# A four-layer graph network on one core: relation scores in rounded halves, a new set-up and new orders on every engine

## The chip, the cores and the metric

The kernel runs on one core of one Trainium2 chip. A core has five engines with queues of their own: TensorE (PE; its weight loads are shown apart as PEld), VectorE (DVE), ScalarE (ACT), GpSimd (POOL) and SyncE (SP), which issues the DMAs here. Each works its queue in order and waits on semaphores. Only PE multiplies matrices; it writes to PSUM, which has eight banks of 128 x 512 float32. The metric is the device time of one execution in microseconds; the median of several runs counts.

## The reference, cut to what matters

128 graphs of 128 nodes with 256 features pass four residual layers, each on `h = relu(layernorm(x))`:

```python
# L0: attention of 8 heads under the adjacency mask, projection, layer norm added to itself
attn = softmax(where(adj == 0, -inf, q @ k.T * scale)); o = (attn @ v) @ w_proj + b_proj
x = x + o + layernorm(o) * gamma + beta
# L1: relation scores
q, k, v = h @ Wq.T, h @ Wk.T, h @ Wv.T
rel = adj.T * (q @ k.T)
rel = rel / norm(rel, axis=2, keepdims=True)
x = x + rel @ v
# L2: graph attention
g = h @ W
e = leaky_relu((g @ a1)[:, :, None] + (g @ a2)[:, None, :], 0.2) * adj
x = x + elu(softmax(e) @ g + beta * g)
# L3
x = x + (adj @ h) @ weight + bias
```

All arrays are float32.

## The kernel before

The graphs go in 64 pairs. The work on a pair is cut into stages, and a loop over steps `t` runs eight streams: in step `t` an engine works on pair `t` in stream 0 (`p0`), pair `t - 1` in stream 1 (`p1`), and so on to `p7`. Each engine has a function `step(t, par, on)` in which its operations stand in an order written out by hand, and `run(eng, step, set_up)` calls the steps; a pair `(t, make)` in its list calls the set-up function `make` ahead of step `t`. Every operation waits for its inputs by a count on a semaphore (`done`), for the last reader of a buffer that it overwrites (`wait_before`), and on PE for its PSUM bank (`bank_free`).

**Products.** A matrix product of two float32 operands is made in one of two ways. `product` (its matmuls stand on L314) takes operands that are split into a rounded high half and a rounded low half (`parts`, float32r) and adds three passes, hi times hi, hi times lo, lo times hi. It makes q, k, v, the projection, g, v1, hw and y, always with 256 or 258 moving columns. The other way is a plain float32 matmul, which appears as two instructions each: scores (L358), heads and their sums (L370, L374), rel times v (L417), u (L488), y_t (L520) and the relation scores (L458), and the transposes, which appear as one.

**The relation scores.** L1 folds Wq and Wk into one matrix when it starts (`fold`, L384), so that rel is h times g with g = w_qk times h. In before, ScalarE copies g out of PSUM as float32 (`g_t`, L650), and PE multiplies:

```python
last = pe.matmul(rel_bank[:, b * N:(b + 1) * N], h_t1_full[:, c, b * N:(b + 1) * N],
                 g_t[:, c, b * N:(b + 1) * N], start=c == 0, stop=c == C - 1)
```

four matmuls of 128 columns for a pair. `h_t1_full` is the float32 copy; its halves `h_t[1]` exist too, for g and v1.

**Normalising.** `moments` (VectorE: L706, L710) takes mean and variance, `inverse_root` (GpSimd: L901, L903) the inverse root, `normalize` (VectorE, L725) makes z. For L3 it is ScalarE instead: VectorE makes a shift, and ScalarE makes h in one operation with scale and bias (L590). PE transposes z, ScalarE makes the high half, VectorE the low one (`relu_lo`).

**The leaky slope.** ScalarE adds the two score vectors (Identity with bias, L612) into `e_sum`, VectorE makes `e_leaky` as the greater of the sum and 0.2 times the sum (L770), GpSimd multiplies with the adjacency (L942).

**Set-up.** SP issues x of pair 0, w_qkv, adj, w_q, w_k, x of pair 1, then the constants (`CONSTS`, the last one gamma) and the late constants (`LATE_CONSTS`, the last one w_out). ScalarE makes the high half of w_qkv in one piece, VectorE the low half. `fold` is called ahead of PE's step 0, `copy_fold` ahead of ScalarE's. VectorE makes the low half of the folded matrix ahead of its step 2, and GpSimd splits the other weights ahead of its step 2 (`next_constants`, `last_constants`).

Of the kernel before, what the change touches and what calls it, by code (L numbers as in the profile page):

```python
# [6 lines left out]
def gnn_stack(nc, x, adj, adj_t, w_qkv, w_proj, b_proj, gamma, beta_ln, w_q, w_k, w_v_t,  # L7
# [4 lines left out]
    ALU = mybir.AluOpType  # L12
# [16 lines left out]
    STREAMS = 8  # L29
# [5 lines left out]
    with ctx:  # L35
# [63 lines left out]
        rstd = sb("rstd", [128, NORMS, 2])  # L99
        shift3 = sb("shift3", [128, 2])  # L100
# [20 lines left out]
        g_t = sb("g_t", [128, C, 2 * N])  # L121
# [7 lines left out]
        e_sum = sb("e_sum", [128, 2, N])  # L129
# [21 lines left out]
        q_bank = mid[:, 2]  # L151
        k_bank = bank4[:]
        v_bank = bank7[:]
        p0_bank = mid[:, 0]
        p1_bank = bank5[:]
        p2_bank = bank7[:]
        p3_bank = bank4[:]
        heads_bank = bank5[:]
        sums_bank = mid[:, 0]
        o_bank = mid[:, 0]  # L160
        z1_bank = bank6[:]
        g_bank = bank6[:]
        v1_bank = bank6[:]
        rel_bank = mid[:, 3]
        rel_v_bank = bank4[:]
        z2_bank = mid[:, 2]
        hw0_bank = bank6[:]
        hw1_bank = mid[:, 2]
        s2_bank = mid[:, 1]
        att_bank = bank4[:]  # L170
        u_bank = mid[:, 1]
        y_t_bank = bank7[:]
        y_bank = bank5[:]
# [5 lines left out]
        mask_made, folded, folded_ready = sem("mask_made"), sem("folded"), sem("folded_ready")  # L179
# [8 lines left out]
        o_hi_ready, o_lo_ready = sem("o_hi_ready"), sem("o_lo_ready")  # L188
        q_psum, k_psum, v0_psum = sem("q_psum"), sem("k_psum"), sem("v0_psum")
# [5 lines left out]
        o_norm_ready, o_psum, o_ready = sem("o_norm_ready"), sem("o_psum"), sem("o_ready")  # L195
# [6 lines left out]
        hw_psum, hw_ready, s2_psum, e_sum_ready = sem("hw_psum"), sem("hw_ready"), sem("s2_psum"), sem("e_sum_ready")  # L202
# [47 lines left out]
        def flat(tile):  # L250
# [9 lines left out]
            (w_q_sb, w_q.rearrange("(c p) n -> p c n", p=128), fold_in),  # L260
            (w_k_sb, w_k.rearrange("(c p) n -> p c n", p=128), fold_in),
# [18 lines left out]
        def _(sp):  # L280
# [4 lines left out]
            for dst, src in CONSTS:  # L285
                sp.dma_start(dst, src).then_inc(const_in, 16)
            for dst, src in LATE_CONSTS:
                sp.dma_start(dst, src).then_inc(late_const_in, 16)

            def step(t, par, load, store):  # L290
                pb, p_out = t - 2, t - 7
# [6 lines left out]
                if store:  # L298
                    i = (par + 7) % 2
# [3 lines left out]
            for t in range(PAIRS + 7):  # L303
                step(t, t % 2, 2 <= t < PAIRS + 2 - 2, t >= 7)
# [4 lines left out]
        def _(pe):  # L309
# [69 lines left out]

            def fold():  # L380
                pe.wait_ge(fold_in, 16 * 2)
                for j in range(C):
                    for c in range(C):
                        last = pe.matmul(bank4[:, j * D:(j + 1) * D], w_q_sb[:, c, j * 128:(j + 1) * 128],  # L384
                                         w_k_sb[:, c, :], start=c == 0, stop=c == C - 1)
                last.then_inc(folded, 1)
                pe.wait_ge(fills_made, 3)
                pe.wait_ge(w_hi_ready, 2)
                pe.wait_ge(w_lo_ready, 1)

            def next_weights():
                pe.wait_ge(const_in, 16 * len(CONSTS))
                pe.wait_ge(split_ready, 2 * len(SPLIT))
                pe.wait_ge(w_lo_ready, 2)
# [6 lines left out]
            def step(t, par, on):  # L401
                p0, p1, p2, p3, p4, p5, p6, p7, p8 = [t - s for s in range(STREAMS + 1)]

                if on[1]:
                    pe.wait_ge(h_lo_ready[0], done(p1))
                    bank_free(pe, (hw_ready, p5, 2), (h_lo_ready[2], p5, 1), (max_ready[2], p2, 1))
                    columns(q_bank, w_qkv_p, 0, h_t[0]).then_inc(q_psum, 1)
                if on[3]:
                    pe.wait_ge(z_ready[1], done(p3))
                    bank_free(pe, (hw_ready, p5, 2), (v1_ready, p4, 1), (g_ready, p4, 1))  # L410
# [580 lines left out]
```

## Time and profile before

| | |
|---|---|
| median of 3 runs | 1473.15 us (1472.97 to 1476.63) |
| the profiled execution | 1474.63 us |
| its span, first to last instruction | 1472.8 us |
| PE, DVE, ACT, POOL busy | 98%, 86%, 77%, 51% of the span |
| granted TensorE clock, mean | 0.995 |

Busy time of an engine is the time in which at least one of its instructions runs; matmuls overlap one another, so their durations don't add up. The chain of work that ended last is PE for 95% of the span.

### The profile page before, as it was taken

What the parts mean: (1) busy time and instruction counts of PE and PEld (TensorE: products, weight loads), DVE (VectorE), ACT (ScalarE), POOL (GpSimd) and SP (SyncE); (2) the same over time, 40 slices, a digit from 0 to 9 for tenths busy, and PEclk for the clock granted to TensorE, in tenths of its full rate; (3) what the DMA queues carried; (4) which work ended last, traced back from release to release, by engine and by line L of the source; (5) the groups of instructions that cost most, each with busy time, mean ns of one, the idle gap of its engine ahead of it and who ended that gap; (6) DMA issues with size and microseconds to landing.
All of it is one profiled execution on the core that took longest, in us unless ns stands there. A gap on an engine that the chain in (4) does not pass through costs nothing.

```text
span 1472.8 us, 47814 instructions
## 1 busy us (share of the span) xinstructions
PE 1438.2 (98%) x16136; PEld 1370.3 (93%) x16136; DVE 1273.4 (86%) x5774; ACT 1134.7 (77%) x2884; POOL 748.4 (51%) x1107
## 2 busy tenths in 40 slices
PE   5999999999999999999999999999999999999996
PEld 5899999999999999999999999999999999999985
DVE  4889988988989889889889889889889889889885
ACT  4778878878877877877877778778778788788753
POOL 3455555555555555555555555555555555555452
PEclk9999999999999999999999999999999999999998
DMA  3000000100000000001001000000001001000000
GB/s 111 17 17 23 31 16 30 31 16 31 30 17 31 30 16 31 28 19 31 24 23 30 23 24 30 24 24 31 23 24 30 23 24 30 19 28 31 9 23 30
DMA packets 38113, 39.90 MB, mean 27 GB/s; under 512 B 2416, under 2 KB 37488, under 8 KB 37872
## 3 DMA queue, kind: packets, MB, share of 16 engines
q1 hardware_dynamic: 37872, 36.84, 7.9%
q8 instruction: 133, 2.18, 0.6%
q14 instruction: 108, 0.88, 0.2%
HBM read 20.05 MB, written 16.78 MB: 25 GB/s over the span
## 4 chain that ended last, share of the span: by engine, by line
PE 95%; DVE 1%; ACT 1%; issue 1%; POOL 0%; DMA 0%; SPq 0%; POOLq 0%; ACTq 0%; DVEq 0%
PE bank L314 34%; PE mid L314 15%; PE bank L349 6%; PE mid L358 5%; PE bank L520 5%; PE bank L370 4%; PE mid L458 4%; PE mid L374 4%; PE bank L330 4%; PE mid L488 4%; PE bank L417 4%; PE mid L330 2%; PE mid L349 2%; PE mid L493 1%; PE mid L527 1%
## 5 line engine op out<-in xcount | busy, mean ns | idle before, releaser
L546 ACT ACTIVATE probs<-masked,neg_max 128x128 f32<-128x128 f32 x1024 | 326.3, 395 | 6.3 <-DVE neg_max L716 6.3
L903 POOL TENSOR_TENSOR rstd<-var_eps,minus_half 128x2 f32<-128x2 f32 x320 | 240.9, 753 | 25.5
L716 DVE CUSTOM_DVE_ANT_0 masked<-mid,mask 128x128 f32<-128x128 f32 x1024 | 234.9, 286 | 6.9 <-issue 6.8
L915 POOL TENSOR_TENSOR xb<-x,b_proj_beta 128x512 f32<-128x512 f32 x64 | 81.9, 1279 | 233.9 <-DVE o_res L828 233.9
L901 POOL TENSOR_TENSOR var_eps<-mean_var,eps 128x2 f32<-128x2 f32 x320 | 63.5, 198 | 243.0 <-DVE mean_var L710 242.7
L706 DVE BATCH_NORM_STATS2 stats<-x 128x6 f32<-128x256 f32 x384 | 143.3, 415 | 0.1
L725 DVE TENSOR_SCALAR z<-x,mean_var,rstd 128x256 f32<-128x256 f32 x384 | 134.5, 405 | 7.1 <-POOL rstd L903 6.7
L946 POOL TENSOR_TENSOR h_t_lo<-h_t_full,h_t_hi 128x512 fp32r<-128x512 f32 x64 | 82.0, 1282 | 79.4 <-ACT h_t_hi L629 79.4
L349 PE MATMUL bank<-ident,probs 128*128 128x128 f32 x768 | 117.6, 276 | 4.9 <-ACT probs L546 4.9
L942 POOL TENSOR_TENSOR e_mask<-e_leaky,adj_sb 128x256 f32<-128x256 f32 x64 | 46.8, 731 | 116.2 <-DVE e_leaky L770 116.2
L370 PE MATMUL bank<-probs_t,v 128*32 128x128 f32 x2048 | 104.5, 276 | 0.3 <-issue 0.3
L770 DVE SCALAR_TENSOR_TENSOR e_leaky<-e_sum 128x256 f32<-128x256 f32 x64 | 27.3, 426 | 88.7 <-ACT e_sum L612 88.7
L374 PE MATMUL mid<-probs_t,ones 128*32 128x128 f32 x2048 | 103.0, 273 | 0.0
L604 ACT ACTIVATE ln_sum<-mid 128x512 f32<-128x512 f32 x64 | 38.2, 597 | 80.5 <-PE mid L374 80.5
L349 PEld LDWEIGHTS bank<-ident,probs 128*128 128x128 f32 x768 | 91.1, 147 | 6.2 <-ACT probs L546 6.2
L710 DVE BATCH_NORM_AGGREGATE mean_var<-stats 128x2 f32<-128x6 f32 x640 | 77.8, 163 | 13.8
L919 POOL TENSOR_TENSOR x3b<-x_up,b_out_less 128x512 f32<-128x512 f32 x64 | 82.6, 1290 | 11.3 <-DVE x L824 11.3
L314 PE MATMUL bank<-w_out_hi,y_t_hi 128*128 128x256 f32 x256 | 79.4, 310 | 6.9 <-DVE y_t_lo L778 6.9
L716 DVE DVE_READ_ACCUMULATOR2_ANT neg_max<- 128x1 f32 x1024 | 84.6, 83 | 0.0
L950 POOL TENSOR_TENSOR o_t_lo<-o_t,o_t_hi 128x512 fp32r<-128x512 f32 x64 | 83.0, 1298 | 3.1 <-ACT o_t_hi L633 3.1
L358 PEld LDWEIGHTS mid<-k_t,q_t 32*128 32x128 f32 x2048 | 63.0, 186 | 22.7 <-issue 20.2
L783 DVE SCALAR_TENSOR_TENSOR x<-bank,inv_norm,x 128x256 f32<-128x256 f32 x128 | 56.1, 480 | 28.8 <-PE bank L417 28.8
(156 smaller groups left out, 5725.8 us busy)
## 6 DMA issues: line engine op xcount, KB each, us to landing
x<-in_x SPq DMA_DIRECT2D x64, 256.0 KB, 2.7
out_x<-x SPq DMA_DIRECT2D x64, 256.0 KB, 2.1
w_qkv_sb<-in_w_qkv SPq DMA_DIRECT2D x1, 768.0 KB, 4.4
w_q_sb<-in_w_q SPq DMA_DIRECT2D x1, 256.0 KB, 4.4
w_k_sb<-in_w_k SPq DMA_DIRECT2D x1, 256.0 KB, 4.6
w_v_sb<-in_w_v_t SPq DMA_DIRECT2D x1, 256.0 KB, 5.8
w_proj_sb<-in_w_proj SPq DMA_DIRECT2D x1, 256.0 KB, 6.0
w_gat_x<-in_w_gat SPq DMA_DIRECT2D x1, 256.0 KB, 7.2
```

The costliest lines, as they stand in the source:

```text
L314: last = pe.matmul(dst, pick_l(lhs_t[a], c), pick_r(rhs[b], c), start=n == 0, stop=n == len(terms) - 1)
L330: last = pe.transpose(dst[:, (c * 2 + b) * N:(c * 2 + b + 1) * N], src[:, b, c * 128:(c + 1) * 128], ident[:])
L349: last = pe.transpose(dst[:, s * N:(s + 1) * N], probs[:, r, s], ident[:])
L358: last = pe.matmul(mid[:, r, s * N:(s + 1) * N], q_t[at, hc, b * N:(b + 1) * N], k_t[at, hc, b * N:(b + 1) * N], start=True, stop=True, ti ...
L370: pe.matmul(heads_bank[at, to], v0[:, b, hc * RG + r], probs_t[:, r, s], start=True, stop=True, tile_position=(0, r * HD))
L374: last = pe.matmul(sums_bank[at, to], ones[:], probs_t[:, r, s], start=True, stop=True, tile_position=(0, r * HD))
L546: last = act.activation(probs[:, r, s], masked[:, r, s], ACT.Exp, scale=-1.0, bias=neg_max[:, r, s:s + 1])
L706: dve.bn_stats(stats[:, k, b], src[:, b]).then_inc(ln_stats[k], 1)
L716: last = dve.tensor_tensor_reduce(out=masked[:, r, s], in0=mid[:, r, s * N:(s + 1) * N], in1=mask[:], scale=1.0, scalar=LARGE, op0=ALU.add ...
L725: last = dve.tensor_scalar(z[k][:, b], src[:, b], mean_var[:, k, b, 0:1], rstd[:, k, b:b + 1], ALU.subtract, ALU.mult)
L903: pool.tensor_tensor(rstd[:, k], var_eps[:, k], minus_half[:], ALU.pow).then_inc(ln_rstd[k], 1)
L950: pool.tensor_tensor(o_t_p[1][:], o_t[:], o_t_p[0][:].bitcast(f32), ALU.subtract).then_inc(o_lo_ready, 1)
```

## The change

- **Relation scores.** g gets halves too (`g_t_p`): ScalarE copies the rounded high half, VectorE subtracts it for the low half (`g_lo_ready`), and PE makes rel with `product`: twelve rounded matmuls of 128 columns in place of four in float32.
- **Leaky slope on ScalarE.** One Prelu with bias and slope makes `e_leaky`; `e_sum` and VectorE's operation go.
- **First z on ScalarE.** VectorE makes a shift of 128x2, and ScalarE makes z of L0 with Identity, scale and bias.
- **Set-up.** w_q and w_k are issued behind the constants. The halves of w_qkv are made in three pieces. `fold_low` (the low half of the folded matrix) and GpSimd's set-up are called ahead of step 0. PE waits ahead of step 0 for the weights, then folds; the folded matrix is made in the bank of the first score group, and step 0's scores wait until it is copied.
- **Orders.** The order on PE, ScalarE, VectorE and GpSimd is written anew, with other banks; the scores of a pair are made in stream 0 of PE (before: 1), z of L1 is transposed in stream 2 (before: 3), rel times v is in stream 3 (before: 4). With `STREAMS = 9` the sum into x4 and its store come one step later.

```diff
-    STREAMS = 8
+    STREAMS = 9
...
-        g_t = sb("g_t", [128, C, 2 * N])
+        g_t_p = parts("g_t", [128, C, 2 * N])
...
-            (w_q_sb, w_q.rearrange("(c p) n -> p c n", p=128), fold_in),
-            (w_k_sb, w_k.rearrange("(c p) n -> p c n", p=128), fold_in),
+        ]
+        FOLD_CONSTS = [
+            (w_q_sb, w_q.rearrange("(c p) n -> p c n", p=128)),
+            (w_k_sb, w_k.rearrange("(c p) n -> p c n", p=128)),
...
             for dst, src in CONSTS:
                 sp.dma_start(dst, src).then_inc(const_in, 16)
+            for dst, src in FOLD_CONSTS:
+                sp.dma_start(dst[:], src).then_inc(fold_in, 16)
...
-                    for b in range(2):
-                        for c in range(C):
-                            last = pe.matmul(rel_bank[:, b * N:(b + 1) * N], h_t1_full[:, c, b * N:(b + 1) * N],
-                                             g_t[:, c, b * N:(b + 1) * N], start=c == 0, stop=c == C - 1)
+                    for b in range(2):
+                        last = product(rel_bank[:, b * N:(b + 1) * N], h_t[1], g_t_p,
+                                       lambda a, c: a[:, c, b * N:(b + 1) * N], lambda a, c: a[:, c, b * N:(b + 1) * N])
...
-            run(pe, step, [(0, fold), (2, next_weights), (4, last_weights)])
+            run(pe, step, [(0, first_weights), (0, value_weights), (0, fold), (3, folded_weights),
+                          (2, next_weights), (4, last_weights)])
...
+                        act.activation(e_leaky[:, b], s2_bank[:, b * N:(b + 1) * N], ACT.Prelu, bias=hw[:, b, D:D + 1], alpha=ALPHA)\
+                           .then_inc(e_leaky_ready, 1)
...
+                    act.activation(flat(g_t_p[0]), g_bank, ACT.Copy).then_inc(g_ready, 1)
...
+                        last = act.activation(z[0][:, b], x0[:, i0, b], ACT.Identity, bias=shift[0][:, b:b + 1],
+                                              scale=rstd[:, 0, b:b + 1])
...
-            run(act, step, [(0, copy_fold)])
+            run(act, step, [(0, first_weights), (0, copy_fold)])
...
+            def fold_low():
+                dve.wait_ge(folded_ready, 2)
+                dve.tensor_tensor(w_qk_p[1][:], w_qk_sb[:], w_qk_p[0][:].bitcast(f32), ALU.subtract)\
+                   .then_inc(folded_lo_ready, 1)
...
-                if on[0]:
-                    normalize(0, p0, x0[:, i0])
...
-                    dve.scalar_tensor_tensor(e_leaky[:], e_sum[:], ALPHA, e_sum[:], ALU.mult, ALU.max).then_inc(e_leaky_ready, 1)
...
+                    dve.tensor_tensor(flat(g_t_p[1]), g_bank, flat(g_t_p[0]).bitcast(f32), ALU.subtract).then_inc(g_lo_ready, 1)
...
-            run(dve, step, [(0, first_constants), (2, next_constants), (2, last_constants)])
+            run(dve, step, [(0, first_constants), (0, fold_low), (2, next_constants), (2, last_constants)])
...
-            run(pool, step, [(2, next_constants), (2, last_constants)])
+            run(pool, step, [(0, next_constants), (0, last_constants)])
```

The order of PE's blocks in one step, with the stream of each:

```text
before: q1 z1T3 rel.v4 scores1 y7 v1 g3 proj2 attT5 rel3 z0T0 z2T4 p3 v1' p2 p0 u5 sumsq3 p1 k0 hw4 heads1 yT6 s2T4
after:  proj2 y7 p3 z0T0 g3 p0 p2 v1' p1 q0 z2T4 rel3 attT5 heads1 u5 k0 sumsq3 hw4 yT6 scores0 z1T2 s2T4 v0 rel.v3
```

(p0 to p3 are the transposes of the four groups of probabilities, stream 1; v1 and v0 are L0's value product in stream 1 or 0, v1' is that of L1, stream 3; T marks transposes.)

## Rows read from the trace of the kernel before

**Rows 1.** The page, part 1: busy us (share of the span) and instructions of each engine.
```profile
PE 1438.2 (98%) x16136; PEld 1370.3 (93%) x16136; DVE 1273.4 (86%) x5774; ACT 1134.7 (77%) x2884; POOL 748.4 (51%) x1107
```

**Rows 2.** Busy time by stretch: us, then each engine; PEclk, DMA share, GB/s.
```profile
122.20:1387.60 1265.40, 1265.40 (x14369) 1211.63 (x14365) 1125.45 (x5127) 1006.18 (x2565) 657.82 (x970) 1.00 0.08 26
722.20:744.40 22.20, 22.20 (x254) 21.26 (x254) 19.74 (x91) 17.65 (x46) 11.53 (x18) 1.00 0.08 26
...
1387.60:1472.80 85.20, 67.75 (x544) 61.44 (x540) 57.50 (x200) 44.52 (x111) 34.77 (x49) 0.92 0.07 23
```

**Rows 3.** Groups of PE, 122.20 to 1387.60: xcount | busy us, mean ns | idle before.
```profile
L458 PE MATMUL mid<-g_t,h_t_full 128*128 128x128 f32 x456 | 60.2, 275 | 0.0
```

**Rows 4.** Timeline of PE in one period: start us, us, line, tiles, xcount.
```profile
710.56 1.06 PE L458 MATMUL mid<-g_t,h_t_full 128*128 128x128 f32 x8
711.45 0.60 PE L330 MATMUL bank<-ident,z 128*128 128x128 f32 x4
```

**Rows 5.** Timeline of PE, a rounded block after a float32 one.
```profile
712.68 0.36 PE L314 MATMUL bank<-w_v_hi,h_t_hi 128*128 128x256 f32 x1
712.88 0.28 PE L314 MATMUL bank<-w_v_lo,h_t_hi 128*128 128x256 f32 x1
...
714.06 0.28 PE L314 MATMUL bank<-w_v_hi,h_t_lo 128*128 128x256 f32 x1
```

**Rows 6.** Timeline of PE's weight loads after the scores.
```profile
704.54 0.19 PEld L314 LDWEIGHTS bank<-w_out_hi,y_t_hi 128*128 128x128 f32 x1
704.65 0.19 PEld L314 LDWEIGHTS bank<-w_out_lo,y_t_hi 128*128 128x128 f32 x1
```

**Rows 7.** Timeline of PE: float32 products of 256 columns, then the scores.
```profile
702.48 1.03 PE L417 MATMUL bank<-v,rel 128*128 128x256 f32 x4
703.44 0.39 PE L358 MATMUL mid<-k_t,q_t 32*128 32x128 f32 x4
```

**Rows 8.** Groups of DVE in one period: xcount | busy us, mean ns | idle.
```profile
L725 DVE TENSOR_SCALAR z<-x,mean_var,rstd 128x256 f32<-128x256 f32 x7 | 2.5, 403 | 0.0
...
L778 DVE TENSOR_TENSOR y_t_lo<-bank,y_t_hi 128x512 fp32r<-128x512 f32 x1 | 0.7, 680 | 0.0
...
L770 DVE SCALAR_TENSOR_TENSOR e_leaky<-e_sum 128x256 f32<-128x256 f32 x1 | 0.4, 427 | 1.4 <-ACT e_sum L612 1.4
```

**Rows 9.** Groups of ACT in one period.
```profile
L590 ACT ACTIVATE h<-x_up,shift,rstd 128x256 f32<-128x256 f32 x2 | 1.1, 608 | 0.0
```

**Rows 10.** Timeline of all engines at the start.
```profile
7.48 3.75 PE L384 MATMUL bank<-w_k_sb,w_q_sb 128*128 128x256 f32 x8 [7.48 <-DMA w_k_sb<-in_w_k]
...
9.13 0.75 DVE L706 BATCH_NORM_STATS2 stats<-x 128x6 f32<-128x256 f32 x2
...
10.33 0.20 POOL L901 TENSOR_TENSOR var_eps<-mean_var,eps 128x2 f32<-128x2 f32 x1 [8.86 <-DVE mean_var L710]
...
11.34 0.73 DVE L725 TENSOR_SCALAR z<-x,mean_var,rstd 128x256 f32<-128x256 f32 x2 [1.17 <-POOL rstd L903]
...
12.46 0.87 PE L330 MATMUL bank<-ident,z 128*128 128x128 f32 x3 [1.22 <-ACT w_qk_hi L542]
```

**Rows 11.** Timeline of SP's DMA queue at the start.
```profile
5.71 0.47 SPq L286 DMA_DIRECT2D gamma_bc<-in_gamma  x1
...
10.05 0.83 SPq L288 DMA_DIRECT2D w_out_sb<-in_w_out  x1
```

**Rows 12.** DMA issues: tensor, count, KB each, median us from issue to landing.
```profile
w_out_sb<-in_w_out SPq DMA_DIRECT2D x1, 256.0 KB, 7.3
...
gamma_bc<-in_gamma SPq DMA_DIRECT2D x1, 128.0 KB, 7.1
```

**Rows 13.** Timeline of POOL, its set-up and the first xb.
```profile
16.92 0.73 POOL L880 TENSOR_TENSOR b_proj_beta<-b_proj_bc,beta_ln_bc 128x256 f32<-128x256 f32 x1
...
25.69 1.27 POOL L915 TENSOR_TENSOR xb<-x,b_proj_beta 128x512 f32<-128x512 f32 x1
```

**Rows 14.** ACT's table loads: count, ns min/median/max, first and last start.
```profile
L535 ACT ACT_TABLE_LOAD  x1: 1283/1283/1283, 0.7 to 0.7; - x1
```

More of the change, by code:

```diff
@@ L99, in gnn_stack @@
         rstd = sb("rstd", [128, NORMS, 2])
+        shift = [sb(f"shift{k}", [128, 2]) for k in range(3)]
         shift3 = sb("shift3", [128, 2])
@@ L401, in step @@
             def step(t, par, on):
[L402 to L410, printed above, removed]
-                    transposes(z1_bank, z[1]).then_inc(h_t_psum[1], 1)
@@ L445, in step @@
                     last.then_inc(o_psum, 1)
+                if on[7]:
+                    pe.wait_ge(y_lo_ready, done(p7))
+                    bank_free(pe, (max_ready[0], p1, 1))
+                    rows(halves(y_bank), y_t_p, w_out_p, 0, D).then_inc(y_psum, 1)
+                if on[1]:
+                    pe.wait_ge(probs_ready[3], done(p1))
+                    bank_free(pe, (x2_ready, p4, 2), (max_ready[3], p1, 1), (q_ready, p1, 1))
+                    transpose_probs(3).then_inc(probs_t_psum[3], 1)
@@ L489, in step @@
                     last.then_inc(u_psum, 1)
+                if on[0]:
+                    pe.wait_ge(h_lo_ready[0], done(p0))
+                    bank_free(pe, (v1_ready, p3, 1), (max_ready[1], p1, 1))
+                    columns(k_bank, w_qkv_p, D, h_t[0]).then_inc(k_psum, 1)
                 if on[3]:
@@ L529, in step @@
                     last.then_inc(s2_psum, 1)
-            run(pe, step, [(0, fold), (2, next_weights), (4, last_weights)])
+                if on[0]:
+                    pe.wait_ge(h_lo_ready[0], done(p0))
+                    bank_free(pe, (hw_ready, p4, 2), (h_lo_ready[2], p4, 1), (h_lo_ready[0], p0, 1))
+                    rows(halves(v_bank), h_t[0], w_qkv_p, 2 * D, D).then_inc(v0_psum, 1)
+                if on[3]:
+                    pe.wait_ge(v1_ready, done(p3))
+                    pe.wait_ge(rel_ready, done(p3))
+                    bank_free(pe, (max_ready[3], p0, 1), (q_ready, p0, 1), (probs_t_ready[3], p1, 1))
+                    for b in range(2):
+                        last = pe.matmul(rel_v_bank[:, b * D:(b + 1) * D], rel[:, b], v1[:, b], start=True, stop=True)
+                    last.then_inc(rel_v_psum, 1)
+            run(pe, step, [(0, first_weights), (0, value_weights), (0, fold), (3, folded_weights),
+                          (2, next_weights), (4, last_weights)])
         @block.scalar
@@ L596, in step @@
                     act.activation(flat(k_t), k_bank, ACT.Copy).then_inc(k_ready, 1)
+                if on[0]:
+                    act.wait_ge(shift_ready[0], done(p0))
+                    wait_before(act, h_t_psum[0], p0)
+                    for b in range(2):
+                        last = act.activation(z[0][:, b], x0[:, i0, b], ACT.Identity, bias=shift[0][:, b:b + 1],
+                                              scale=rstd[:, 0, b:b + 1])
+                    last.then_inc(z_ready[0], 1)
                 if on[5]:
```

606 lines of the change are left out of this document (300 added, 306 removed).

## The prediction

> **What bounds the kernel now.** I read the page first: PE is busy 98% of the span [rows 1]. Busy PE time counts overlapping matmuls, so I next asked for busy time by stretch. From 122.20 to 1387.60 us PE is busy for all of 1265.40 us [rows 2]. The groups of that stretch say how long that is in pairs: the relation scores (L458) stand there 456 times, 8 to a pair, so 57 pairs, and the idle time ahead of them is 0.0 [rows 3]. One pair costs 1265.40 / 57 = 22.20 us, and PE waits for nobody. The other engines have room in such a period: VectorE 19.74 us, ScalarE 17.65, GpSimd 11.53 [rows 2]. So in the middle of the run only the time that PE itself needs counts. 64 x 22.20 = 1420.8 us of the 1472.8; the other 52 us are filling and draining the pipeline. I cost three things: PE's work for a pair, the start, the end.
>
> What PE's work costs can't be read from a matmul's own duration (275 ns, but four start in 0.44 us); it is the distance from one start to the next.
>
> **The relation scores.** Now a pair has 4 float32 products of 128 columns; each shows as two passes, 8 in all. They start at 710.56 and the next group at 711.45 [rows 4]: 0.89 us, 111 ns a pass. After the change there are 12 passes in rounded float32, still with 128 columns. No row of before shows such a pass; those on record have 256 columns. Their starts go from 712.88 to 714.06 in ten steps: 118 ns [rows 5]. What sets it? Each pass loads its own 128 weights. PE comes out of an idle moment, and the first two loads of the rounded kind start 108 ns apart, 704.54 and 704.65 [rows 6], with no earlier matmul in the way. So a load takes some 108 to 118 ns, whatever the matmul that follows streams, and halving the columns doesn't halve the pass. Bounds: below, 108 ns, or 1.30 us for the twelve (+0.41 a pair); above, the dearest single pass on record, the float32 one of 256 columns, 0.96 / 4 = 240 ns [rows 7], or 2.88 us (+1.99 a pair). I take 118 ns, the row of the same type and the same weights: 12 x 0.118 = 1.41 us, +0.52 us a pair. The passes saved by arithmetic (three instead of four) don't arrive, because PE pays for weight loads, and those go from 8 to 12.
>
> The Trainium skill (TensorE: Matmul & The Clock Gate, LDWEIGHTS) says that a load takes its columns divided by 1.2 ns, 107 ns for 128; the spacing of 108 ns [rows 6] agrees, and by that rule the twelve would cost an estimated 1.28 us.
>
> **The order on PE.** The other products are the same in number and shape. Dense blocks change place, and a change of kind costs something where the four-way tiles (scores, heads) begin and end; both orders enter and leave them twice, so I put nothing. Switches between float32 and rounded blocks go from four to eight a pair; the first pass after float32 work takes 0.20 us, 712.68 to 712.88 [rows 5], 0.08 over its row, but starts early by nearly as much, so I put 0.02 us a pair and keep 0 to 0.09.
>
> Together +0.54 us a pair, a period of 22.74 us; over 64 pairs +34.6 us. With the low bound, 0.41, it is +26.
>
> **The other engines.** VectorE loses the first z (2 x 403 ns) and the leaky slope (427), gains the low half of g, priced as the one of y (680) [rows 8], and a shift of two columns: 19.74 - 1.23 + 0.68 = 19.2 us, and a little. ScalarE gains two z of 128x256, priced as its h (608 each, [rows 9]): 17.65 + 1.2 = 18.9; its Prelu takes the place of the Identity, one for one and of the same shape. GpSimd stays. All lie below 22.7, so what they gain or lose is covered by PE, and if PE had no such work it would be worth under a microsecond a pair. Whether the new order makes PE wait I checked by laying out one period in sequence with these prices: the narrowest handover is rel times v, whose bank is freed only when VectorE has masked score group 3, about 1 us of room. The x load and the store on SP wait for z and for x4 as before, once a period of 22 us.
>
> **The start.** It is said to have the first z ahead, so I followed what each queue holds in front of it. Now x0 statistics start at 9.13 and z is transposed at 12.46 [rows 10]; the fold of the two relation weights on PE (3.75 us from 7.48) is done by then. In the change all set-up calls of step 0 stand in front of step 0 on their engines:
> - SP issues the two fold weights after the five constants, in the place gamma has now. Gamma was issued at 5.71 and takes 7.1 us [rows 11, 12]: they land near 12.8. Fold to 16.6; two copies on ScalarE and the subtraction (the low half) on VectorE, about 2 us, to 18.6. Only then may VectorE start the moments of x0, ending near 19.8.
> - GpSimd makes all its constants before its first inverse root. The set-up takes 16.92 to 25.69 now, five instructions for each of two groups [rows 13], so 4.4 us a group. The second waits for the last constant, issued at 10.05 and 7.3 us under way: 17.35 [rows 11, 12]. It ends near 21.7; the root, 1.0 us (10.33 to 11.34 [rows 10]), at 22.7.
> - The shift, then z on ScalarE in two of 0.6: near 24.0, against 12.46: 11.5 us later.
> From there to the first scores the chain is the same (transposes, halves, q and k, copies), and the next pairs are bound by the chain through maximum, exponentials, transposes and heads, as now. Nothing lies in front of that first z to hide its delay. I take 11.5 us; bounds: 5 (if the weights land early and the roots are waited for alone) and 14.
>
> **The end.** After 1387.60 the last pairs take 85.2 us of which PE works 67.75 [rows 2]; the same chain of stages is left, with g's low half more (0.68) and the leaky hop from ScalarE to VectorE less (0.43); the ninth stream moves the sum into x4 and its store to a later step and adds no work. I put 0, and 6 either way for a new order in a chain that is no longer dense.
>
> **Sum.** 34.6 + 11.5 + 0 = +46 us on a profiled execution of 1474.63 us: 1521. That execution is 1.5 us above the median of the runs, 1473.15: 1519 against it. With the pass in the middle between its load (108) and its row (118), 113 ns, 4 us less: I say 1515.
>
> **Rivals.**
> *A rounded pass of 128 columns is half of one of 256.* Place: the twelve passes. At 59 ns they cost 0.71 us, 0.18 less than now: -12 us, which the start takes back: 1474, no change. It decides from 58 ns a pass; under that the kernel is faster. For it: 256 columns in 118 ns is nearly a column a cycle at 2.4 GHz. Against it: the loads 108 ns apart [rows 6], and the float32 passes of 128 columns, which load as much and take 111. The Trainium skill (same page, Back-to-back issue gap) gives 56 ns for an isolated pass of 128 columns, and by that the time would be an estimated 1472; the same section speaks of 81 ns when loads and matmuls alternate, an estimated 1491. No row here is under 108.
> *A rounded pass of 128 columns falls to float32 pace.* Then each is two passes, 222 ns, 2.66 us for twelve: +1.77 a pair, +113, and with the start and the switches near 1599. For it: no rounded product in the kernel has under 256 columns. Against it: the kind of load is the same, and nothing in the trace ties pace to columns in that way.
> *The new order makes PE wait.* If the mask of group 3 is late or Prelu needs a table that isn't loaded (one load is on record, 1283 ns [rows 14]; two a pair would bring ScalarE to 21.5), PE waits some 0.3 to 0.7 us a pair: 1535 to 1560. For it: 1 us of room. Against it: sums well under the period.
> *The start isn't later, and the end is shorter.* If z0 comes as early as now, 1503; that is still slower.
>
> **How the numbers follow.** Forecast 0.70 (its own range 1500 to 1530); float32 pace 0.10; waiting PE 0.08; half pass 0.07, split between the same and faster; 0.05 for an end or block switches that give back over 40 us, which no row supports. So slower by over 0.3% (about what measurements here tell from no change) 0.88, within 0.3% 0.05, faster 0.07. The range reaches from a cheap load with an early start, 26 + 5 - 6 = +25, or 1498, to a PE that waits 0.45 us a pair, 1515 + 29 = 1544; left out are the two rivals on the pass's pace, the rest, and the worst of the waits, about 2 in 10.
>
> **What would show it.** In the profile after: rel's block twelve passes in 1.3 to 1.4 us with starts 108 to 118 ns apart; a period near 22.7 with PE idle 0; the first z transposed near 24 us; the fold beginning near 13; VectorE near 19.3 and ScalarE near 18.9 us a period. It is wrong if the passes start 60 or 220 ns apart, if PE shows idle time in the middle, or if the first z comes before 15 us.

## The result, and the profile after

The changed kernel takes 1507.48 us (median of 4 runs, 1507.21 to 1508.00) against 1473.37 us for the kernel before on the same chip (4 runs, 1472.97 to 1476.63): a ratio of 1.0223 [1.0211, 1.0235]. It is slower, and 7.5 us faster than the 1515 forecast. The profiled execution took 1507.36 us, its span is 1505.6 us.

The page says little about it: PE's share falls by one point [rows 1], because it waits at the start.

```profile
PE 1459.8 (97%) x16392; PEld 1399.2 (93%) x16392; DVE 1262.1 (84%) x5712; ACT 1184.1 (79%) x3014; POOL 755.3 (50%) x1107
```

The busy time by stretch says more. The columns are the stretch, its length and the busy time of PE, PEld, DVE, ACT and POOL, then the granted clock, the DMA share and GB/s. The first stretch runs from the first yT block of PE to the 58th, as the one of before does; the second is one period in it. Under it is one of PE's groups in the first stretch.

```profile
138.64:1423.80 1285.16, 1285.16 (x14594) 1238.56 (x14593) 1114.24 (x5069) 1048.73 (x2677) 663.37 (x967) 1.00 0.08 25
823.30:845.85 22.55, 22.55 (x259) 21.73 (x258) 19.57 (x90) 18.42 (x48) 11.65 (x18) 1.00 0.09 25
1423.80:1505.60 81.80, 66.01 (x542) 59.12 (x540) 58.32 (x203) 42.87 (x110) 36.24 (x52) 0.95 0.07 24
...
L323 PE MATMUL bank<-g_t_hi,h_t_hi 128*128 128x128 f32 x228 | 64.6, 283 | 0.0
```

PE is again busy for the whole stretch, with no idle time ahead of the relation scores. Four products of this form are one pair, so 228 are 57 pairs, and 1285.16 / 57 = 22.55 us a pair, against 22.20 [rows 2, 3]. The other engines stay below that.

With the marks of [rows 2, 10] the 32.8 us by which the span grew (1505.6 - 1472.8) fall into four pieces that add up to it:

| piece | before | after | difference |
|---|---|---|---|
| from the start to z0 transposed | 12.46 | 24.50 | +12.04 |
| from there to the first yT block | 109.74 | 114.14 | +4.40 |
| 57 periods | 1265.40 | 1285.16 | +19.76 |
| from the 58th yT block to the end | 85.20 | 81.80 | -3.40 |

The timeline of PE shows the relation scores of one period (start, us, engine, line, tiles), which answers to [rows 4]:

```profile
829.37 0.60 PE L339 MATMUL bank<-ident,z 128*128 128x128 f32 x4
829.72 0.31 PE L323 MATMUL bank<-g_t_hi,h_t_hi 128*128 128x128 f32 x1
829.87 0.28 PE L323 MATMUL bank<-g_t_lo,h_t_hi 128*128 128x128 f32 x1
829.98 0.27 PE L323 MATMUL bank<-g_t_hi,h_t_lo 128*128 128x128 f32 x1
...
830.98 0.28 PE L323 MATMUL bank<-g_t_hi,h_t_lo 128*128 128x128 f32 x1
831.09 0.41 PE L477 MATMUL mid<-ident,att_norm 128*128 128x128 f32 x2
```

From the second pass to the last are ten steps in 1.11 us: 111 ns each, exactly the float32 pass of 128 columns of before. The twelve take 831.09 - 829.72 = 1.37 us against 0.89, +0.48 us a pair.

The timeline of the start (all engines, lines left out; in brackets the idle time before and what ended it) answers to [rows 10]:

```profile
13.61 3.37 PE L400 MATMUL mid<-w_k_sb,w_q_sb 128*128 128x256 f32 x8 [13.61 <-DMA w_k_sb<-in_w_k]
...
17.44 0.61 POOL L920 TENSOR_TENSOR b_out_less<-b_out_bc,ones 128x256 f32<-128x256 f32 x1 [1.53 <-DMA w_out_sb<-in_w_out]
17.50 0.59 ACT L564 ACTIVATE w_qk_hi<-mid 128x512 fp32r<-128x512 f32 x1
...
18.20 0.95 DVE L710 TENSOR_TENSOR w_qk_lo<-w_qk_sb,w_qk_hi 128x512 fp32r<-128x512 f32 x1 [9.54 <-ACT w_qk_hi L564]
...
19.95 0.15 DVE L739 BATCH_NORM_AGGREGATE mean_var<-stats 128x2 f32<-128x6 f32 x1
20.93 1.26 POOL L926 TENSOR_TENSOR w_out_lo<-w_out_sb,w_out_hi 128x512 fp32r<-128x512 f32 x1
22.14 0.20 POOL L931 TENSOR_TENSOR var_eps<-mean_var,eps 128x2 f32<-128x2 f32 x1
22.42 0.70 POOL L933 TENSOR_TENSOR rstd<-var_eps,minus_half 128x2 f32<-128x2 f32 x1
23.16 0.16 DVE L796 SCALAR_TENSOR_TENSOR shift<-mean_var,rstd 128x2 f32<-128x2 f32 x1 [3.06 <-POOL rstd L933]
23.35 1.09 ACT L665 ACTIVATE z<-x,shift,rstd 128x256 f32<-128x256 f32 x2 [5.26 <-DVE shift L796]
24.50 1.12 PE L339 MATMUL bank<-ident,z 128*128 128x128 f32 x4 [7.53 <-ACT z L665]
```

There are two queues ahead of the root. VectorE waits for the fold and has the moments at 20.1 us. GpSimd works through its constants until 22.1 us, and only then takes the root. The later one counts: here GpSimd.

The waits with the largest sums (engine and line, what ended them, us in total, times, longest) all lie with other engines than PE:

```profile
POOL rel_sq L978 <- DVE rel L783: 310.4, 64, 5.0
...
DVE masked L745 <- issue: 80.5, 64, 3.3
...
DVE rel L783 <- PE bank L323: 71.0, 63, 1.2
```

Since PE has no gap in the middle, none of them costs time there.

### The profile page after: what moved, and what is told of

The parts are those of the page before. It is cut to its first block, busy times and chain, and to the rows that moved or that the text cites. A ratio compares the mean times of both kernels' runs of the same rounds, so it can differ in the third digit from the quotient of the medians.

```text
span 1505.6 us, 48400 instructions
## 1 busy us (share of the span) xinstructions
PE 1459.8 (97%) x16392; PEld 1399.2 (93%) x16392; DVE 1262.1 (84%) x5712; ACT 1184.1 (79%) x3014; POOL 755.3 (50%) x1107
## 4 chain that ended last, share of the span: by engine, by line
PE 93%; issue 2%; ACT 1%; DVE 1%; POOL 1%; DMA 1%; SPq 1%; POOLq 0%; DVEq 0%; ACTq 0%
PE bank L323 29%; PE mid L323 23%; PE bank L339 6%; PE mid L367 5%; PE mid L490 4%; PE bank L379 4%; PE bank L383 4%; PE bank L358 4%; PE mid L358 4%; PE bank L511 4%; PE mid L544 4%; PE bank L499 1%; PE mid L477 1%; PE bank L532 1%; ACT probs L568 1%
## 5 line engine op out<-in xcount | busy, mean ns | idle before, releaser
L323 PE MATMUL mid<-h_t_hi,w_qkv_hi 128*128 128x256 f32 x512 | 161.1, 315 | 1.4 <-DVE h_t_lo L760 1.4
L323 PE MATMUL mid<-h_t_hi,w_qkv_lo 128*128 128x256 f32 x512 | 144.0, 281 | 0.0
L323 PE MATMUL mid<-h_t_lo,w_qkv_hi 128*128 128x256 f32 x512 | 143.9, 281 | 0.0
L339 PE MATMUL bank<-ident,z 128*128 128x128 f32 x768 | 119.6, 278 | 11.5 <-ACT z L665 7.5
L339 PEld LDWEIGHTS bank<-ident,z 128*128 128x128 f32 x768 | 86.3, 142 | 20.2 <-ACT z L665 7.9
L383 PE MATMUL bank<-probs_t,ones 128*32 128x128 f32 x2048 | 102.9, 273 | 0.0
L323 PEld LDWEIGHTS mid<-h_t_hi,w_qkv_hi 128*128 128x128 f32 x512 | 98.4, 192 | 4.2 <-DVE h_t_lo L760 1.8
L323 PEld LDWEIGHTS mid<-h_t_lo,w_qkv_hi 128*128 128x128 f32 x512 | 97.7, 191 | 1.7
L323 PEld LDWEIGHTS mid<-h_t_hi,w_qkv_lo 128*128 128x128 f32 x512 | 97.3, 190 | 0.0
L760 DVE SCALAR_TENSOR_TENSOR h_t_lo<-bank,h_t_hi 128x512 fp32r<-128x512 f32 x128 | 84.5, 660 | 5.9 <-ACT h_t_hi L596 5.4
```

The lines of the kernel that those rows point to most:

```text
L323: last = pe.matmul(dst, pick_l(lhs_t[a], c), pick_r(rhs[b], c), start=n == 0, stop=n == len(terms) - 1)
L339: last = pe.transpose(dst[:, (c * 2 + b) * N:(c * 2 + b + 1) * N], src[:, b, c * 128:(c + 1) * 128], ident[:])
L383: last = pe.matmul(sums_bank[at, to], ones[:], probs_t[:, r, s], start=True, stop=True, tile_position=(0, r * HD))
L760: dve.scalar_tensor_tensor(h_t[k][1][:].rearrange("p c n -> p (c n)"), bank, 0.0, h_t[k][0][:].rearrange("p c n -> p (c n)").bitcast(f32), ...
```

## The experiments

My theory: two costs, independent of each other. A pass on PE costs the load of its weights, so three rounded products for one float32 product mean twelve loads for eight; and the set-up ahead of the first z makes the start late by GpSimd's queue. The rivals stand with each run. Eleven kernels ran, in four groups; each was compared with the kernel before on its own chip (medians 1475.90, 1474.47, 1475.95 and 1475.64 us; 1473.37 us on that of the changed kernel). So two medians of the table that lie within some 2.6 us of each other aren't told apart by it. In the table the last three columns, in us, are from the traces.

| kernel | median us | ratio to before [interval] | period | z0 transposed | first yT |
|---|---|---|---|---|---|
| changed kernel | 1507.48 | 1.0223 [1.0211, 1.0235] | 22.55 | 24.50 | 138.64 |
| rel_float32 | 1481.24 | 1.0031 [1.0018, 1.0044] | 22.13 | 24.31 | 136.29 |
| rel_alone | 1504.75 | 1.0201 [1.0184, 1.0219] | 22.65 | 12.65 | 124.08 |
| rel_two_passes | 1479.41 | 1.0027 [1.0016, 1.0038] | 22.10 | 24.88 | 136.89 |
| rel_256_columns | 1508.94 | 1.0234 [1.0213, 1.0255] | 22.58 | 24.02 | 138.68 |
| half_weights | 1474.49 | 0.9992 [0.9981, 1.0003] | 21.99 | 23.67 | 134.75 |
| setup_before | 1496.18 | 1.0146 [1.0130, 1.0163] | 22.55 | 13.17 | 126.49 |
| pool_setup_late | 1504.66 | 1.0204 [1.0189, 1.0219] | 22.55 | 22.88 | 136.68 |
| fold_early | 1507.29 | 1.0219 [1.0204, 1.0234] | 22.55 | 23.54 | 136.89 |
| vector_z_leaky | 1512.50 | 1.0252 [1.0237, 1.0267] | 22.55 | 24.09 | 140.99 |
| float32_and_setup | 1469.40 | 0.9961 [0.9949, 0.9973] | 22.13 | 13.58 | 125.99 |
| first_z_ahead | 1463.97 | 0.9927 [0.9914, 0.9939] | 22.13 | 7.23 | 120.07 |

### The passes of the relation scores

**rel_float32** undoes the three passes and keeps the rest of the change.

```diff
-                        last = product(rel_bank[:, b * N:(b + 1) * N], h_t[1], g_t_p,
-                                       lambda a, c: a[:, c, b * N:(b + 1) * N], lambda a, c: a[:, c, b * N:(b + 1) * N])
+                        for c in range(C):
+                            last = pe.matmul(rel_bank[:, b * N:(b + 1) * N], h_t1_full[:, c, b * N:(b + 1) * N],
+                                             g_t[:, c, b * N:(b + 1) * N], start=c == 0, stop=c == C - 1)
...
-                if on[3]:
-                    dve.wait_ge(g_ready, done(p3))
-                    dve.tensor_tensor(flat(g_t_p[1]), g_bank, flat(g_t_p[0]).bitcast(f32), ALU.subtract).then_inc(g_lo_ready, 1)
```

> The changed kernel with the relation scores as four float32 products again (g copied once, no low half of g); set-up, orders and the work on ScalarE stay. Theory of weight loads: PE pays about 108 ns for each pass of 128 columns, so eight float32 passes (0.89 us) replace twelve rounded ones (1.29 us): period 22.55 - 0.40 = 22.15 us, time 1507.5 - 64 x 0.40 = 1482. Rival, the new order costs the time: period stays near 22.5, time near 1507.

**rel_alone** is the other side: the kernel before with the three passes and g's low half alone, the block moved behind the transposes of the third z.

```diff
-                            last = pe.matmul(rel_bank[:, b * N:(b + 1) * N], h_t1_full[:, c, b * N:(b + 1) * N],
-                                             g_t[:, c, b * N:(b + 1) * N], start=c == 0, stop=c == C - 1)
+                        last = product(rel_bank[:, b * N:(b + 1) * N], h_t[1], g_t_p,
+                                       lambda a, c: a[:, c, b * N:(b + 1) * N], lambda a, c: a[:, c, b * N:(b + 1) * N])
...
+                if on[3]:
+                    dve.wait_ge(g_ready, done(p3))
+                    dve.tensor_tensor(flat(g_t_p[1]), g_bank, flat(g_t_p[0]).bitcast(f32), ALU.subtract).then_inc(g_lo_ready, 1)
```

> The kernel before with the three rounded passes for the relation scores alone (the block stands behind the transposes of the third z, VectorE makes the low half of g). Weight loads: period 22.20 + 0.40 = 22.60, time 1473.4 + 26 = 1499; up to 1505 if the longer chain through the low half of g makes PE wait in an order not made for it. Rival, the new order costs the time: 1473.

Two rows by stretch, of 57 periods each, the first from rel_float32 and the second (in a fence of its own) from rel_alone:

```profile
136.29:1397.51 1261.22, 1261.22 (x14366) 1214.43 (x14365) 1074.20 (x5012) 1048.83 (x2677) 663.52 (x967) 1.00 0.08 26
```

```profile
124.08:1415.42 1291.34, 1291.27 (x14597) 1236.94 (x14593) 1161.52 (x5183) 1007.43 (x2565) 657.41 (x968) 1.00 0.08 25
```

The periods are 22.13 and 22.65. So the passes cost 0.42 us a pair in the changed order (22.55 - 22.13) and 0.45 in the old one (22.65 - 22.20), and the rest of the change takes 0.07 to 0.10 us a pair off PE's time. The passes alone made the kernel before 2.0% slower; without them 0.3% of the loss is left. The new orders were not run by themselves.

What sets a pass's price? Three kernels tell its possible causes apart. **rel_two_passes** leaves out a third of the products (h's low half times g), so that eight rounded passes stand where twelve did:

```diff
-                        last = product(rel_bank[:, b * N:(b + 1) * N], h_t[1], g_t_p,
-                                       lambda a, c: a[:, c, b * N:(b + 1) * N], lambda a, c: a[:, c, b * N:(b + 1) * N])
+                        at = slice(b * N, (b + 1) * N)
+                        for n, (c, part) in enumerate([(c, part) for c in range(C) for part in range(2)]):
+                            last = pe.matmul(rel_bank[:, at], h_t[1][0][:, c, at], g_t_p[part][:, c, at],
+                                             start=n == 0, stop=n == 2 * C - 1)
```

> The changed kernel without the third pass (low half of h times high half of g is left out of the sum): eight rounded passes in place of twelve. Weight loads: 4 x 108 ns less a pair, period 22.12, time 1480, the same as with eight float32 passes. Rival, a pass costs the columns that it streams (54 ns): 0.21 us less a pair, time 1494.

**rel_256_columns** streams both entries' g through each entry's weights, twice the columns for the same loads, and reads only the half that belongs to it:

```diff
-                        last = product(rel_bank[:, b * N:(b + 1) * N], h_t[1], g_t_p,
-                                       lambda a, c: a[:, c, b * N:(b + 1) * N], lambda a, c: a[:, c, b * N:(b + 1) * N])
+                        last = product(rel_bank[:, b * 2 * N:(b + 1) * 2 * N], h_t[1], g_t_p,
+                                       lambda a, c: a[:, c, b * N:(b + 1) * N], lambda a, c: a[:, c])
```

> The changed kernel with twelve passes of 256 columns in place of 128 (each graph's h also meets the other graph's g; that half of the result isn't read). Weight loads: a pass goes from 108 to the 118 ns of the other rounded products, 12 x 10 ns = 0.12 us more a pair, period 22.67, time 1515. Rival, a pass costs its columns (54 ns for 128): 0.64 us more a pair, time 1548.

**half_weights** keeps the columns and takes half of the weights, which leaves out half of the rows of the product:

```diff
-                        last = product(rel_bank[:, b * N:(b + 1) * N], h_t[1], g_t_p,
-                                       lambda a, c: a[:, c, b * N:(b + 1) * N], lambda a, c: a[:, c, b * N:(b + 1) * N])
+                        last = product(rel_bank[0:64, b * N:(b + 1) * N], h_t[1], g_t_p,
+                                       lambda a, c: a[:, c, b * N:b * N + 64], lambda a, c: a[:, c, b * N:(b + 1) * N])
```

> The changed kernel, with 64 instead of 128 weights in each of the twelve passes of the relation scores; 128 columns still stream, and the lower 64 of the 128 rows of each relation product are left out (the bank keeps what stood there). Theory (a pass costs its weight load): a load of half as many weights takes half as long, as the heads' loads of 32 weights come every 27 ns; the twelve fall from 1.37 us to about 0.7 us, the period from 22.55 to about 21.9, and the time to about 1464. Rival (a pass costs a fixed 110 ns, whatever it loads and streams): the period stays at 22.55, the time at 1507.

The timeline of PE in these three, second and last pass of the block and what follows, in this order:

```profile
814.71 0.28 PE L472 MATMUL bank<-g_t_lo,h_t_hi 128*128 128x128 f32 x1
...
815.38 0.28 PE L472 MATMUL bank<-g_t_lo,h_t_hi 128*128 128x128 f32 x1
815.50 0.29 PE L479 MATMUL mid<-ident,att_norm 128*128 128x128 f32 x1
```

```profile
830.97 0.28 PE L323 MATMUL bank<-g_t_lo,h_t_hi 128*128 128x256 f32 x1
...
832.10 0.28 PE L323 MATMUL bank<-g_t_hi,h_t_lo 128*128 128x256 f32 x1
832.22 0.38 PE L477 MATMUL mid<-ident,att_norm 128*128 128x128 f32 x2
```

```profile
809.17 0.23 PE L323 MATMUL bank<-g_t_lo,h_t_hi 128*64 128x128 f32 x1
...
809.79 0.23 PE L323 MATMUL bank<-g_t_hi,h_t_lo 128*64 128x128 f32 x1
809.85 0.40 PE L477 MATMUL mid<-ident,att_norm 128*128 128x128 f32 x2
```

Two lines more, of the changed kernel: the sums of squares, whose passes stream one single column through 128 weights, and what follows them:

```profile
835.72 0.47 PE L499 MATMUL bank<-ones,rel_sq 128*128 128x1 f32 x3
836.05 0.36 PE L323 MATMUL bank<-w_gat_hi,h_t_hi 128*128 128x258 f32 x1
```

Eight passes: six steps in 0.67 us, 112 ns each. Twice the columns: ten steps in 1.13 us, 113 ns. Half the weights: ten steps in 0.62 us, 62 ns. One column: three passes in 0.33 us, 111 ns each. With 128 weights, then, the number of passes and their weights set the price; doubling the columns adds 2 ns a pass and 0.03 us a pair (0.12 was expected). What holds a pass of 64 weights at 62 ns, its load or the 128 columns that still stream, these runs don't tell. Both rivals fall, that columns count (22.55 would have become over 23) and that a pass has a fixed price. Of half_weights the time missed what I expected, 1464, by 10 us, and the period tells most: 21.99 us is 0.56 less than the changed kernel's, 64 x 0.56 = 36 us, or 1471.6, and its profiled execution took 1470.53. Its median is 4 us above that; its runs go from 1470.53 to 1476.16 us, with mean granted clocks between 0.988 and 0.998. What set the clock in them stays open.

### The start

**setup_before** puts the set-up back where the kernel before has it (the halves of w_qkv stay in three pieces).

```diff
+            for dst, src in FOLD_CONSTS:
+                sp.dma_start(dst[:], src).then_inc(fold_in, 16)
             sp.dma_start(x0[:, 1], x_pairs[1]).then_inc(x_in[1], 16)
...
-            for dst, src in FOLD_CONSTS:
-                sp.dma_start(dst[:], src).then_inc(fold_in, 16)
...
-            run(pe, step, [(0, first_weights), (0, value_weights), (0, fold), (3, folded_weights),
+            run(pe, step, [(0, fold), (0, first_weights), (0, value_weights), (3, folded_weights),
...
-            run(dve, step, [(0, first_constants), (0, fold_low), (2, next_constants), (2, last_constants)])
+            run(dve, step, [(0, first_constants), (2, fold_low), (2, next_constants), (2, last_constants)])
...
-            run(pool, step, [(0, next_constants), (0, last_constants)])
+            run(pool, step, [(2, next_constants), (2, last_constants)])
```

> The changed kernel with the set-up placed as in the kernel before: SP issues the two fold weights right behind the first half of x0, TensorE folds before its first z, and VectorE's low half of the fold and GpSimd's constants come two steps later. Theory (the start is late because the set-up stands ahead of the first z on VectorE and GpSimd): z0 is transposed near 13 us instead of 24.5, the period stays 22.55, and the time falls by about 11 us, 1507.5 to about 1496. Rival (the fill of the pipeline has room that swallows the delay, and the late first yT comes from the order): 1505 to 1508.

**pool_setup_late** makes only the last of these edits (GpSimd's), **fold_early** all but the last.

> The changed kernel, with only GpSimd's own constants moved back by two steps. Two delays stand side by side in the start: GpSimd's constants (end at 22.1 us) and the fold with its low half on VectorE ahead of the moments (moments end near 20.1). Theory (both are late, GpSimd last): the root then waits for VectorE, starts near 20.1, and only 2 us come back: about 1505.5. Rival (GpSimd alone makes the start late): 11 us come back, about 1496.

> The changed kernel, with only the fold's side moved back: its two weights are issued early, TensorE folds before the first z, VectorE's low half comes two steps later; GpSimd's constants stay ahead of the first root. Theory (GpSimd's constants end the wait last): the root still starts near 22 us, the time stays at 1507, within 1.5 us. Rival (the late fold is what makes the start late): about 1496.

The timeline of the start, first of setup_before, then of pool_setup_late, then of fold_early:

```profile
7.47 3.46 PE L400 MATMUL mid<-w_k_sb,w_q_sb 128*128 128x256 f32 x8 [7.47 <-DMA w_k_sb<-in_w_k]
...
9.62 0.20 POOL L931 TENSOR_TENSOR var_eps<-mean_var,eps 128x2 f32<-128x2 f32 x1 [8.15 <-DVE mean_var L739]
...
13.17 0.63 PE L339 MATMUL bank<-ident,z 128*128 128x128 f32 x4 [2.24 <-ACT z L665]
```

```profile
20.52 0.19 POOL L931 TENSOR_TENSOR var_eps<-mean_var,eps 128x2 f32<-128x2 f32 x1 [19.05 <-DVE mean_var L739]
...
22.88 1.11 PE L339 MATMUL bank<-ident,z 128*128 128x128 f32 x4 [5.38 <-ACT z L665]
```

```profile
19.88 1.26 POOL L926 TENSOR_TENSOR w_out_lo<-w_out_sb,w_out_hi 128x512 fp32r<-128x512 f32 x1
21.10 0.19 POOL L931 TENSOR_TENSOR var_eps<-mean_var,eps 128x2 f32<-128x2 f32 x1
```

In setup_before the root starts at 9.62, z0 is transposed 11.3 us earlier than in the changed kernel, the first yT block comes 12.2 us earlier, and the time falls by 11.3 us (1507.48 - 1496.18): nothing in the fill swallows a late start. With GpSimd's constants moved alone the root waits for VectorE instead, starts at 20.52 and gives 2.8 us (expected 2); with the fold moved alone GpSimd still ends late, and the time stays. Neither delay is the cause by itself; each stands behind the other, and only moving both brings the 11 us. In fold_early the first yT block comes 1.75 us earlier (136.89 against 138.64) and the last stretch is that much longer:

```profile
1422.04:1505.60 83.56, 67.92 (x542) 61.06 (x540) 58.30 (x203) 42.96 (x110) 36.27 (x52) 0.91 0.07 24
```

The granted clock is 0.91 there, against 0.95 in the changed kernel's 81.80 us. In two kernels with float32 passes and one order, rel_float32 and first_z_ahead, the same two values go with 81.89 and 80.61 us, so the clock may account for some 1.3 of the 1.8 us. That it does isn't shown.

### The engines beside PE

**vector_z_leaky** puts the first z and the leaky slope back on VectorE, in the changed order.

```diff
-                        act.activation(e_leaky[:, b], s2_bank[:, b * N:(b + 1) * N], ACT.Prelu, bias=hw[:, b, D:D + 1], alpha=ALPHA)\
-                           .then_inc(e_leaky_ready, 1)
+                        act.activation(e_sum[:, b], s2_bank[:, b * N:(b + 1) * N], ACT.Identity, bias=hw[:, b, D:D + 1])\
+                           .then_inc(e_sum_ready, 1)
...
+                    normalize(0, p0, x0[:, i0])
...
+                    dve.scalar_tensor_tensor(e_leaky[:], e_sum[:], ALPHA, e_sum[:], ALU.mult, ALU.max).then_inc(e_leaky_ready, 1)
```

> The changed kernel, with the first z and the leaky slope back on VectorE (ScalarE then writes the sum, VectorE the slope), in the changed order. Theory (TensorE alone bounds the steady part, both engines have room): period 22.55, time 1507.5 give or take 3 us. VectorE goes to about 20.3 us of work a period, ScalarE to about 17.7. Rival (the move to ScalarE is what keeps TensorE free of waits, VectorE with g's low half would be late): a period over 22.8, over 1522.

One period by stretch in it:

```profile
817.40:839.95 22.55, 22.55 (x259) 21.73 (x258) 20.32 (x93) 17.43 (x45) 11.70 (x17) 1.00 0.08 25
```

The period is the same, with VectorE at 20.32 and ScalarE at 17.43 us: in the middle the move is worth nothing, as PE sets the pace. The time is 5 us longer all the same, 2 more than I had allowed. The first yT block is 2.35 us later (140.99), though z0 is transposed 0.4 us earlier, and the last stretch is 2.7 us longer. So the move does help, in the fill and the drain, where PE isn't dense. I read it as the longer chain from engine to engine; no run shows that, or tells z from the slope.

### A kernel that beats both

**float32_and_setup** joins the edits of rel_float32 and setup_before, and keeps the new orders and ScalarE's z and slope.

> The changed kernel with both costs taken out: relation scores as float32 products (8 passes of 111 ns) and the set-up placed as in the kernel before; the new orders, ScalarE's z and leaky slope stay. Theory (the two costs add, and what is left of the change is a small gain): 1481 less 11, about 1470, some 4 us under the kernel before, ratio 0.997; period 22.13. Rival (the two overlap, since the late start only matters where the steady part is dense): 1476 to 1481.

**first_z_ahead** goes on from there: VectorE takes the moments of x0 and ScalarE its z before either touches w_qkv, the fold comes one step later, and its copies three steps.

```diff
             def first_weights():
                 pe.wait_ge(fills_made, 3)
+                pe.wait_ge(z_ready[0], 1)
+                transposes(z0_bank, z[0]).then_inc(h_t_psum[0], 1)
                 pe.wait_ge(w_lo_ready, 2)
...
             def first_constants():
+                dve.wait_ge(x_in[0], 16)
+                moments(0, 0, x0[:, 0])
+                shift_first(0)
...
-            run(act, step, [(0, first_weights), (0, copy_fold)])
+            run(act, step, [(0, first_weights), (3, copy_fold)])
```

> As float32_and_setup, and the first z truly ahead of everything on all three engines: moments, shift and z of x0 before the halves of w_qkv are made, z0 transposed near 7.5 us, the fold on TensorE one step later and its copies two more. Theory (whatever the first z gains, the end gains): about 5 us under float32_and_setup, about 1465, ratio 0.993. Rival (w_qkv's halves bound the first q and k, not z): the first halves of w_qkv take until about 12 us whoever comes first, and the time is that of float32_and_setup within 2 us, 1470.

The start of PE in first_z_ahead:

```profile
7.23 1.09 PE L339 MATMUL bank<-ident,z 128*128 128x128 f32 x4 [7.23 <-ACT z L560]
10.54 0.55 PE L323 MATMUL mid<-h_t_hi,w_qkv_hi 128*128 128x256 f32 x1 [2.23 <-DVE h_t_lo L774]
10.89 0.41 PE L323 MATMUL mid<-h_t_lo,w_qkv_hi 128*128 128x256 f32 x1
...
18.43 1.89 PE L399 MATMUL bank<-w_k_sb,w_q_sb 128*128 128x256 f32 x8
20.16 0.60 PE L358 MATMUL mid<-ident,probs 128*128 128x128 f32 x4
```

The two costs add: 1507.48 less 26.2 (rel_float32) less 11.3 (setup_before) is 1470.0, and the joint kernel takes 1469.40, 0.39% under the kernel before [0.27%, 0.51%]. Most of that gain is the shorter period, 64 x (22.20 - 22.13) = 4.5 us. With the first z at 7.23 us instead of 13.58 another 5.4 us go, to 1463.97, 0.73% under it [0.61%, 0.86%]. The rival, that w_qkv's halves would hold the first products back to 12 us, falls: they start at 10.54.

## Why the prediction held, step by step

- **What bounds the kernel.** Right. PE is busy for all of the 1285.16 us in the middle, and no experiment that left its passes alone changed the period.
- **A pass costs its load, not its columns.** Right for rounded passes of 128 weights with 128 or 256 columns, shown by the three kernels above. The price was 118 ns in the sum and 113 in the forecast; it measured 111. The row it was taken from [rows 5] was of the right type but came out 7 ns high; the float32 passes of the same shape [rows 4] had the price to the nanosecond. That agreement is partly luck, and the prediction leans on it against the rival of the half pass: over 256 columns a float32 pass takes 216 ns (the fold in first_z_ahead, 1.73 us for eight), so at 128 its columns alone would ask for an estimated half, 108 ns, which can't be told from the load. By the Trainium skill (TensorE: Matmul & The Clock Gate, LDWEIGHTS) 64 weights would load in an estimated 53 ns; half_weights shows 62 ns a pass, and half of the 111 would be 56. The 56 and 81 ns that the Trainium skill gives for a pass of 128 columns (same page, Back-to-back issue gap) were not seen in any block of 128 weights here.
- **The sum for a pair.** Mis-sized: +0.54 us (0.48 at 113 ns) against 0.35 measured. The passes gave +0.48 (0.52 predicted). The sum put the switch into rounded work at nearly nothing: a first pass 0.08 us dearer that starts nearly as much earlier. Here it does start some 0.08 earlier, since the four transposes in front take 0.35 us ahead of it (829.37 to 829.72) and 0.44 ahead of float32 passes, as in rel_float32:

```profile
814.41 0.60 PE L339 MATMUL bank<-ident,z 128*128 128x128 f32 x4
814.85 1.06 PE L471 MATMUL bank<-g_t,h_t_full 128*128 128x128 f32 x8
```

  But the first pass takes only 0.15 us, 0.04 more than the others. The two transposes behind take 0.34 us in place of 0.31. 0.48 - 0.08 + 0.02 is the 0.42 by which the period differs from rel_float32's. The order of PE, put at +0.02 with these switches, measured -0.07 to -0.10 with all else of the change. In part that is rel times v: with the scores behind it it takes 0.96 us to the next start [rows 7], with the projection behind it 0.67 (841.81 to 842.48 in the changed kernel); of the 0.29 saved the projection's dearer first pass takes back 0.19 (0.31 us, 842.48 to 842.79). The period is thus the term that was mis-sized, by 0.19 us a pair.
- **The other engines.** Right: VectorE 19.57 us a period (19.3 predicted), ScalarE 18.42 (18.9), and PE covers both. The narrow handover to rel times v cost nothing.
- **The start.** Right in its mechanism and nearly in size: z0 transposed at 24.50 (24.0 predicted), 12.0 us later (11.5). The fold began at 13.61 (near 13), GpSimd ended its constants at 22.1 (21.7) after waiting for w_out until 17.44 (17.35). "From there to the first scores the chain is the same" held (7.85 us, against 8.12 before); to the first yT block it is 4.4 us longer. Of that some 1.7 are the passes (rel_alone: 124.08 - 12.65 = 111.43, against 109.74 before) and most of the rest the new order, which with float32 passes takes 112.0 to 112.8. A part goes with the clock, which falls once more between 40.3 and 43.8 us (last section): with the same passes and order and without that fall the stretch is 113.3 to 113.8 us (setup_before, fold_early, pool_setup_late) in place of 114.1.
- **The end.** Put at 0, measured -3.4, inside its bounds of 6. The granted clock was 0.92 in it before and 0.95 after; from the two kernels named under fold_early I estimate 1 us of the 3.4 for that. What gave the rest wasn't tested.
- **The rivals.** Half pass: 111 ns, not 59. Float32 pace: no. A PE that waits: no idle time in the middle. A start that isn't later: it is, by 12.0.
- **The sum.** It was +46, and +32.8 came. The 57 dense periods were put 11.0 us too high (57 x 0.54 = 30.8 against 19.8) and the start 0.5 too low; fill and drain, where the sum had the other seven periods, 3.8 us, came to 4.4 - 3.4 = 1.0. So the errors hardly cancel one another, and nearly all make the sum too high. Taking 113 ns in place of 118 had removed 4 us of this.

## What to carry to other kernels

Price a matmul by the distance to the next start and ask what sets it. In these rows a pass takes the longer of two things, its load (111 ns for 128 weights, with 1 or 128 columns) and its columns (216 ns for 256 in float32). Here it was the load, so three rounded passes lose to a float32 product's two at 128 columns (0.33 us against 0.22), and win only where the columns are the longer part (at 256, 3 x 0.113 to 0.118 or 0.34 to 0.35 us, against 0.43 for a float32 product of the fold, 20.16 - 18.43 = 1.73 us for four in first_z_ahead). Where one engine was dense, moving work between the others changed nothing in the middle; its effect was in fill and drain. Set-up that stood ahead of the first input in an engine's queue arrived in the end nearly in full (11.3 us of time for 11.3 us at the first z). If two queues make the same start late, moving one shows little (2.8 and 0.2 us here), so move both before concluding.

## What the runs showed of the hardware beyond that

- 128 and 256 columns cost nearly the same in rounded passes with 128 weights each: 111 and 113 ns; with 64 weights and 128 columns a pass costs 62. Yet blocks of before with 256 columns and 128 weights take 118 [rows 5]. What makes these 5 ns dearer stays open.
- The clock's column and the pace of the first products don't agree. In the changed kernel PE stands idle from 17.0 to 24.5 us and the granted clock falls to half, the lower of its two levels (1.2 of 2.4 GHz). The columns are the stretch, its length, PE's busy time, the granted clock, the DMA share and GB/s:

```profile
17.00:24.50 7.50, 0.00 (x1) 0.69 0.00 0
24.50:30.00 5.50, 4.09 (x18) 0.50 0.00 0
30.50:40.00 9.50, 6.25 (x69) 1.00 0.10 28
40.30:43.80 3.50, 3.45 (x16) 0.51 0.03 7
```

Its first products of q and k then start 0.21 us apart and go to 0.12 at 30.15 us. The kernel before shows 1.00 for its first products, and they start 0.21 us apart as well (15.33 to 18.74, sixteen steps):

```profile
12.40:20.50 8.10, 5.93 (x28) 1.00 0.34 84
```

  first_z_ahead's do too (10.89 to 13.46, twelve steps). So the late start didn't cost more through the clock in the first products: PE is slow there in all of them. It may have a little later: after a stretch in which PE works 6.25 of 9.50 us the changed kernel's clock falls again, to 0.51 (last row), and the products there start 0.21 us apart (41.47 to 43.61, ten steps). The kernel before shows no such fall: its granted clock is 1.00 up to 1387.60 us.
- The fold's eight passes take 3.37 us as PE's first work in the changed kernel, and 1.73 in first_z_ahead, where the products of q, k and v run ahead of it.
